# One activation-table set for all of ScalarE's functions in a two-layer graph attention kernel

## The chip, the cores and the metric

The kernel runs on one core of a Trainium2 chip. The metric is the device time of one execution in microseconds (us). The engines are named as in the profile: PE is TensorE (PEld its weight loads), DVE is VectorE, ACT is ScalarE, POOL is GpSimd, SP is SyncE, whose queue issues the plain DMAs.

## What is computed

Two layers, each an attention over a sparse graph of 2048 nodes with 256 features, a residual and a layer norm, all in float32:

```
q, k, v = x @ Wq.T, x @ Wk.T, x @ Wv.T
scores  = where(adj.T, q @ k.T, -1e30)
attn    = where(adj.T, softmax(scores, axis=1), 0)
x       = layernorm(x + attn @ v)          # eps 1e-5; done twice, with two sets of weights
```

An edge is there with probability 0.000977, so a node has two neighbours on average.

## The kernel before

The 2048 rows are 16 tiles of 128, handled as 8 pairs (p = 0 to 7) per layer. Dense scores are not computed. At the start (0 to about 62 us) PE packs the adjacency bits, DVE reads neighbour lists out of them, and POOL gathers neighbour rows with indirect DMAs. Each tile has two direct neighbour slots (xd, line 314, two gathers per tile) and one tile of "overflow" rows (xo, line 318, one gather) that holds the third and further neighbours.

One pair then goes through these steps, with lines of the kernel before:

1. PE turns two tiles of x (L935), ACT copies the result to xt (L371), PE multiplies by M = Wq^T Wk (L944), ACT copies it to Q (L380). In layer 0 the pairs 0 to 3 of layer 1 are prepared in this way inside the loop at p = 4 to 7, the next three behind the loop and the last at p = 0 of layer 1.
2. PE expands Q to the overflow edges (L1009); DVE multiplies and sums Q with xd and xo (L709, L716): the scores.
3. PE scatters edge scores to slots (L1021), DVE masks them and takes the maximum (L733, L740), ACT does the exponentials (exps, L416) and scales the first neighbour's row (first_row, L424); DVE adds the second (both_rows, L755).
4. PE takes the maximum to the edges (L1030), DVE subtracts (L747), ACT does the exponential (prob, L431) and scales own_t by it (weight, L435).
5. "Sums": PE adds both_rows and the weighted overflow rows (L1044, L1046), 8 matmuls in two passes each. ACT copies them to y_sb (L443), PE multiplies by Wv^T (L1056), DVE adds the residual (L775).
6. Layer norm: DVE computes mean and variance (L782, L790). ACT computes 1/sqrt(var + eps) as exp(-0.5 * ln(var + eps)): the logarithm at L451, the exponential (root) at L454. DVE makes off_mean (L799) and ACT scales the rows with Identity (L462). The very last but one tile is scaled by DVE (L806).

The steps are written out by hand for each engine and run in that order, with semaphores between the engines. ACT's order in one turn of the loop is: y_sb of pair p-1, X of p-3, xt, exps, first_row, prob, weight of p, logarithm and root of p-2, Q. At p = 2 of layer 0 copies of own_t (L392) and M (L366) follow, at p = 3 the copy of WvT (L366), for which PE waits before its next sums. Behind each layer's loop stands a tail with the norms of the last pairs. SP stores a pair's rows when it is normed, and POOL's gathers for layer 1 wait for the store of all rows of layer 0. From the fifth tile of layer 1 on (AHEAD = 4) a tile's gathers also wait for DVE's products of the tile four before.

ACT's functions on this path are Copy, Abs, Exp, Ln and Identity. The kernel before loads no table by name; the builder puts ACT_TABLE_LOAD instructions where it finds them needed, and their line is that of the ACTIVATE behind them.

A branch at each engine's end (too_many) handles graphs that overflow the lists; these inputs don't enter it.

Of the kernel before, what the change touches and what calls it, by code (L numbers as in the profile page):

```python
# [49 lines left out]
def edges_and_dense(nc, x, adj, wq, wk, wv, out):  # L50

    ctx = ExitStack()
    with ctx:
# [309 lines left out]
        def _(act):  # L363
            def weights(n, bank, into, nth):
                act.wait_ge(s["m_ps"], nth)
                act.activation(into[:, n, :, :], PS[:, bank, :].rearrange("p (h d) -> p h d", h=H), ACT.Copy).then_inc(s["m_sb"], 1)  # L366

            def rows_turned(z):

                act.wait_ge(s["xt_ps"], z + 1)  # L370
                act.activation(xt[:, z % 2, :, :, :], PS[:, 6, :].rearrange("p (j h n) -> p j h n", j=2, h=H),  # L371
                               ACT.Copy).then_inc(s["xt_sb"], 1)
# [16 lines left out]
            def own_turned(c):  # L389
# [3 lines left out]
                               ACT.Copy).then_inc(s["own_t_sb"], 1)  # L393

            weights(0, 4, M, 1)
            rows_turned(0)
            for z in range(1, 4):
# [4 lines left out]
            own_turned(0)  # L402
            own_turned(1)
            weights(0, 5, WvT, 2)
            for z in range(4, PAIRS):
                rows_turned(z)
# [58 lines left out]
            for layer in range(LAYERS):  # L465
                for p in range(PAIRS):
                    z = turned_for(layer, p)
                    if among(p - 1):
                        summed(layer, p - 1)
                    if among(p - 3):  # L470
                        normal(layer, p - 3)
                    if z is not None:
                        rows_turned(z)
                    exponents(layer, p)
                    first_rows(layer, p)
                    if layer == 0 and p == 1:
                        distances(1)
                    overflow_weights(layer, p)
                    if among(p - 2):
                        roots(layer, p - 2)  # L480
                    if z is not None:
                        queries(z)
                    if layer == 0 and p == 2:
                        own_turned(2)
                        own_turned(3)
                        weights(1, 7, M, 3)
                    if layer == 0 and p == 3:
                        weights(1, 6, WvT, 4)
# [692 lines left out]
```

## Time and profile before

| | us |
|---|---|
| median of 3 runs | 311.3 |
| lowest and highest | 307.36 and 314.35 |
| the profiled execution, its time | 310.94 |
| its span, first to last instruction | 309.1 |
| mean granted TensorE clock, share of full speed | 0.797 |
| ACT busy | 139.9 |
| DVE busy | 132.5 |
| POOL busy | 94.4 |

The span is what the profile shows; the execution's own time has 1.8 us more around it. Busy time of an engine is summed over its instructions, and says nothing on what waited for what. For that the timeline gives each instruction's start and duration, and in brackets how long its engine had been idle before it and whose signal ended that. Ends of matmuls are modelled, so an interval on PE is best read from start to start. A granted clock of 1.00 is 2.4 GHz, of 0.50 it is 1.2 GHz.

### The profile page before, as it was taken

What the parts mean: (1) busy time and instruction counts of PE and PEld (TensorE: products, weight loads), DVE (VectorE), ACT (ScalarE), POOL (GpSimd) and SP (SyncE); (2) the same over time, 40 slices, a digit from 0 to 9 for tenths busy, and PEclk for the clock granted to TensorE, in tenths of its full rate; (3) what the DMA queues carried; (4) which work ended last, traced back from release to release, by engine and by line L of the source; (5) the groups of instructions that cost most, each with busy time, mean ns of one, the idle gap of its engine ahead of it and who ended that gap; (6) DMA issues with size and microseconds to landing.
All of it is one profiled execution on the core that took longest, in us unless ns stands there. A gap on an engine that the chain in (4) does not pass through costs nothing.

```text
span 309.1 us, 3691 instructions
## 1 busy us (share of the span) xinstructions
PE 186.0 (60%) x1110; PEld 158.4 (51%) x1110; DVE 132.5 (43%) x671; ACT 139.9 (45%) x311; POOL 94.4 (31%) x115
## 2 busy tenths in 40 slices
PE   1739699640185879298878528650583285957640
PEld 1527587530174767197767426450473184946520
DVE  1229557010097780716874201240185063567430
ACT  1012143400124282739999772210245274688884
POOL 3457102777300036000000007776047315610000
PEclk9999685995556678879999968776599559597965
DMA  8999200433200004110011123333013204311112
GB/s 222 325 311 347 88 0 19 103 107 106 77 0 0 3 25 104 42 34 3 33 35 37 34 68 90 108 104 104 4 35 104 69 33 136 89 49 34 36 36 71
DMA packets 20982, 24.92 MB, mean 81 GB/s; under 512 B 2016, under 2 KB 17888, under 8 KB 20960
## 3 DMA queue, kind: packets, MB, share of 16 engines
q0 software_dynamic: 4608, 12.59, 15.0%
q1 hardware_dynamic: 16352, 12.06, 13.0%
q8 instruction: 11, 0.18, 0.2%
q14 instruction: 11, 0.09, 0.1%
HBM read 20.45 MB, written 4.19 MB: 80 GB/s over the span
## 4 chain that ended last, share of the span: by engine, by line
PE 33%; ACT 23%; issue 19%; another core or an unknown queue 16%; DVE 8%; ACTq 0%; DVEq 0%
PE PS L944 8%; PE PS L1056 7%; ACT L451 5%; PE PS L1044 3%; PE PS L1046 3%; PE PS L1009 3%; ACT first_row L424 3%; ACT exps L416 2%; PE PS L935 2%; ACT weight L435 2%; ACT L454 2%; ACT y_sb L443 2%; DVE X L775 1%; PE PS L918 1%
## 5 line engine op out<-in xcount | busy, mean ns | idle before, releaser
L1056 PE MATMUL PS<-WvT,y_sb 128*128 128x256 f32 x128 | 41.4, 456 | 33.0 <-ACT y_sb L443 32.3
L314 POOL DMA_INDIRECT xd<-x_rows,d_row x32 | 30.6, 957 | 98.6 <-DMA x_rows<-X 62.7
L1044 PE MATMUL PS<-ident,both_rows 128*128 128x128 f32 x128 | 32.6, 346 | 25.1 <-DVE both_rows L755 11.7
L944 PE MATMUL PS<-M,xt 128*128 128x256 f32 x128 | 39.5, 463 | 11.7 <-ACT xt L371 8.6
L1056 PEld LDWEIGHTS PS<-WvT,y_sb 128*128 128x128 f32 x128 | 26.0, 222 | 39.8 <-ACT y_sb L443 35.4
L775 DVE SCALAR_TENSOR_TENSOR X<-PS,inv,X 128x256 f32<-128x256 f32 x32 | 15.4, 483 | 66.9 <-PE PS L1056 62.2
L1044 PEld LDWEIGHTS PS<-ident,both_rows 128*128 128x128 f32 x128 | 26.2, 250 | 26.9 <-issue 19.5
L944 PEld LDWEIGHTS PS<-M,xt 128*128 128x128 f32 x128 | 28.4, 233 | 18.3 <-ACT xt L371 9.9
L314 POOL DMA_INDIRECT xd<-in_x,d_row x32 | 30.5, 955 | 18.5 <-DVE d_row L581 9.4
L709 DVE CUSTOM_DVE_ANT_0 prod<-Q,xd,d_none 128x256 f32<-128x256 f32 x64 | 28.4, 481 | 8.4 <-DMA xd<-x_rows,d_row 8.4
L318 POOL DMA_INDIRECT xo<-in_x,e_row x16 | 15.2, 952 | 54.5 <-DVE e_row L671 50.3
L1046 PE MATMUL PS<-weight,xo 128*128 128x128 f32 x128 | 31.5, 337 | 0.0
L416 ACT ACTIVATE exps<-slots,neg_top 128x18 f32<-128x18 f32 x32 | 9.6, 302 | 48.0 <-issue 26.4
L380 ACT ACTIVATE Q<-PS 128x512 f32<-128x512 f32 x16 | 9.5, 592 | 43.2 <-PE PS L944 21.8
L1046 PEld LDWEIGHTS PS<-weight,xo 128*128 128x128 f32 x128 | 25.9, 251 | 0.0
L716 DVE CUSTOM_DVE_ANT_0 prod<-PS,xo 128x256 f32<-128x256 f32 x32 | 13.4, 419 | 17.9 <-remote 16.3
L443 ACT ACTIVATE y_sb<-PS 128x512 f32<-128x512 f32 x16 | 9.5, 591 | 24.9 <-PE PS L1046 16.3
L451 ACT ACT_TABLE_LOAD x16 | 20.5, 1283 | 0.3
L454 ACT ACT_TABLE_LOAD x16 | 20.5, 1283 | 0.3
L1030 PEld LDWEIGHTS PS<-neg_top,own 128*128 128x128 f32 x64 | 11.1, 222 | 15.6 <-issue 13.5
L1009 PE MATMUL PS<-Q,own 128*128 128x256 f32 x64 | 18.9, 429 | 0.0
L1030 PE MATMUL PS<-neg_top,own 128*128 128x1 f32 x64 | 9.6, 254 | 14.0 <-issue 13.3
(125 smaller groups left out, 303.9 us busy)
## 6 DMA issues: line engine op xcount, KB each, us to landing
adj_words<-in_adj SPq DMA_DIRECT2D x4, 1024.0 KB, 7.1
X<-in_x SPq DMA_DIRECT2D x2, 1024.0 KB
x_rows<-X SPq DMA_DIRECT2D x7, 256.0 KB, 2.1
out<-X SPq DMA_DIRECT2D x7, 256.0 KB
W<-in_L_gnn_Wq SPq DMA_DIRECT2D x2, 256.0 KB
W<-in_L_gnn_Wk SPq DMA_DIRECT2D x2, 256.0 KB
xd<-in_x,d_row POOLq DMA_INDIRECT x32
W<-in_L_gnn_Wv SPq DMA_DIRECT2D x2, 256.0 KB
```

What stands on the lines that cost most here:

```text
L314: pool.indirect_dma_start(xd[:, t, k, :], None, rows, bass.IndirectOffsetOnAxis(ap=d_row[:, t, k:k + 1], axis=0)).then_inc(d_in[t], 16)
L416: act.activation(exps[:, n % 2, j, :], slots[:, n % 2, j, :], ACT.Exp, bias=neg_top[:, n % 2, j:j + 1], scale=-1.0, accum_out=total[:, t:t ...
L451: act.activation(log_var[:, :], moment[:, n % 2, :, 1], ACT.Ln, bias=eps[:, 0:1]).then_inc(s["logged"], 1)
L454: act.activation(root[:, n % 2, :], log_var[:, :], ACT.Exp, scale=-0.5).then_inc(s["rooted"], 1)
L709: dve.tensor_tensor_reduce(out=prod[:, i, :], in0=Q[:, t, :], in1=xd[:, t, k, :], op0=ALU.mult, op1=ALU.add, scale=-1.0, scalar=d_none[:, ...
L775: dve.scalar_tensor_tensor(out=X[layer + 1][:, t, :], in0=projected_into(j), scalar=inv[:, t:t + 1], in1=X[layer][:, t, :], op0=ALU.mult, ...
L944: last = nc.tensor.matmul(PS[:, 7, j * D:j * D + D], xt[:, z % 2, j, h, :], M[:, z // PAIRS, h, :], start=(h == 0), stop=(h == H - 1))
L1009: last = nc.tensor.matmul(expanded(n, j), own[:, 2 * p + j, :], Q[:, 2 * p + j, :], start=True, stop=True)
L1030: last = nc.tensor.matmul(edge_tops(n)[:, j:j + 1], own[:, 2 * p + j, :], neg_top[:, n % 2, j:j + 1], start=True, stop=True)
L1044: nc.tensor.matmul(PS[:, 4, at_h:at_h + P], both_rows[:, n % 2, j, h * P:h * P + P], ident[:, :], start=True, stop=False)
L1046: last = nc.tensor.matmul(PS[:, 4, at_h:at_h + P], xo[:, t, h * P:h * P + P], weight[:, n % 2, j, :], start=False, stop=True)
L1056: last = nc.tensor.matmul(projected_into(j), y_sb[:, n % 2, j, h, :], WvT[:, layer, h, :], start=(h == 0), stop=(h == H - 1))
```

## The change

ACT's program gets one statement at its head. It loads a table set by name, the one that holds logarithm, exponential and the copies, absolute value and identity.

```diff
@@ -364,6 +364,8 @@
             def weights(n, bank, into, nth):
                 act.wait_ge(s["m_ps"], nth)
                 act.activation(into[:, n, :, :], PS[:, bank, :].rearrange("p (h d) -> p h d", h=H), ACT.Copy).then_inc(s["m_sb"], 1)
+
+            act.preload_act_table_set("natural_log_exp_and_others")
 
             def rows_turned(z):
```

All lines behind it are two further down in the changed kernel (L451 becomes L453). What the builder makes of it is seen in ACT's order of instructions. At the head of ACT's program, before:

```order
L362 UNCONDITIONAL_BRANCH
L366 ACT_TABLE_LOAD
L366 ACTIVATE M<-PS 128x512
L371 ACTIVATE xt<-PS 128x512 x2
L380 ACTIVATE Q<-PS 128x512
```

The same place in the changed kernel:

```order
L362 UNCONDITIONAL_BRANCH
L368 ACT_TABLE_LOAD
L366 ACTIVATE M<-PS 128x512
L373 ACTIVATE xt<-PS 128x512 x2
L382 ACTIVATE Q<-PS 128x512
```

There is one load at the head in both, and it stands before the first wait in both. On ACT at the end of the turn p = 7 of layer 0 and in the tail behind it, before:

```order
L435 ACTIVATE weight<-own_t,prob 128x128 x2
L451 ACT_TABLE_LOAD
L451 ACTIVATE log_var<-moment,eps 128x2
L454 ACT_TABLE_LOAD
L454 ACTIVATE root<-log_var 128x2
L380 ACTIVATE Q<-PS 128x512
L462 ACTIVATE X<-X,off_mean,root 128x256 x2
L443 ACTIVATE y_sb<-PS 128x512
L451 ACT_TABLE_LOAD
L451 ACTIVATE log_var<-moment,eps 128x2
L454 ACT_TABLE_LOAD
L454 ACTIVATE root<-log_var 128x2
```

The same place in the changed kernel:

```order
L437 ACTIVATE weight<-own_t,prob 128x128 x2
L453 ACTIVATE log_var<-moment,eps 128x2
L456 ACTIVATE root<-log_var 128x2
L382 ACTIVATE Q<-PS 128x512
L464 ACTIVATE X<-X,off_mean,root 128x256 x2
L445 ACTIVATE y_sb<-PS 128x512
L453 ACTIVATE log_var<-moment,eps 128x2
L456 ACTIVATE root<-log_var 128x2
```

The loads before the logarithm and before the root are gone, at all 16 places where the two stand, 8 in each layer. Nothing else on the path of these inputs is added, removed or moved, on ACT or on another engine.

## Rows read from the trace of the kernel before

**Rows 1.** The page, part 1 (busy us, share, instructions) and part 4 (chain)

```profile
PE 186.0 (60%) x1110; PEld 158.4 (51%) x1110; DVE 132.5 (43%) x671; ACT 139.9 (45%) x311; POOL 94.4 (31%) x115
...
PE 33%; ACT 23%; issue 19%; another core or an unknown queue 16%; DVE 8%; ACTq 0%; DVEq 0%
```

**Rows 2.** Lines L451, L454: ns min/median/max, first and last start us

```profile
L451 ACT ACT_TABLE_LOAD  x16: 1283/1283/1283, 110.6 to 301.0; - x16
...
L454 ACT ACT_TABLE_LOAD  x16: 1283/1283/1283, 112.2 to 302.6; - x16
```

**Rows 3.** Timeline, layer 0, p = 5: start us, us, engine, line, operation, [idle before]

```profile
148.77 0.69 ACT L435 ACTIVATE weight<-own_t,prob 128x128 f32<-128x128 f32 x2
...
149.48 1.28 ACT L451 ACT_TABLE_LOAD   x1
...
150.77 0.30 ACT L451 ACTIVATE log_var<-moment,eps 128x2 f32<-128x2 f32 x1
...
151.01 0.39 PE L1046 MATMUL PS<-weight,xo 128*128 128x128 f32 x2
...
152.97 0.59 ACT L443 ACTIVATE y_sb<-PS 128x512 f32<-128x512 f32 x1
...
153.61 1.13 PE L1056 MATMUL PS<-WvT,y_sb 128*128 128x256 f32 x4 [0.91 <-ACT y_sb L443]
```

**Rows 4.** Timeline, layer 0, p = 2 to 4

```profile
114.27 3.78 PE L898 MATMUL PS<-W 128*128 128x256 f32 x8 [0.65 <-ACT own_t L392]
...
130.32 0.58 ACT L366 ACTIVATE WvT<-PS 128x512 f32<-128x512 f32 x1
...
130.95 0.80 PE L1044 MATMUL PS<-ident,both_rows 128*128 128x128 f32 x2 [4.99 <-ACT WvT L366]
...
134.53 1.68 PE L1009 MATMUL PS<-Q,own 128*128 128x256 f32 x4
...
140.83 0.38 PE L1044 MATMUL PS<-ident,both_rows 128*128 128x128 f32 x2
...
142.62 1.03 PE L1009 MATMUL PS<-Q,own 128*128 128x256 f32 x4
```

**Rows 5.** Timeline, layer 0, p = 6, p = 7 and the tail

```profile
162.22 1.13 PE L1056 MATMUL PS<-WvT,y_sb 128*128 128x256 f32 x4 [1.78 <-ACT y_sb L443]
...
171.81 1.99 PE L1056 MATMUL PS<-WvT,y_sb 128*128 128x256 f32 x8 [2.75 <-ACT y_sb L443]
...
175.41 1.99 PE L944 MATMUL PS<-M,xt 128*128 128x256 f32 x8 [1.61 <-ACT xt L371]
...
179.03 1.28 ACT L451 ACT_TABLE_LOAD   x1
```

**Rows 6.** Timeline, layer 1, the first two bursts of gathers, a later y_sb

```profile
185.15 0.95 POOL L314 DMA_INDIRECT xd<-x_rows,d_row  x1 [62.67 <-DMA x_rows<-X]
...
197.42 3.59 PE L944 MATMUL PS<-M,xt 128*128 128x256 f32 x8
...
214.14 0.95 POOL L318 DMA_INDIRECT xo<-x_rows,e_row  x1 [0.30 <-issue]
...
218.88 0.60 ACT L380 ACTIVATE Q<-PS 128x512 f32<-128x512 f32 x1 [15.03 <-remote]
...
241.61 0.95 POOL L318 DMA_INDIRECT xo<-x_rows,e_row  x1 [0.30 <-issue]
...
244.78 0.60 ACT L443 ACTIVATE y_sb<-PS 128x512 f32<-128x512 f32 x1 [8.42 <-remote]
...
266.64 0.60 ACT L443 ACTIVATE y_sb<-PS 128x512 f32<-128x512 f32 x1 [0.52 <-PE PS L1046]
```

**Rows 7.** Timeline of PE, layer 1, L1056 behind the loads of p = 5 and p = 7

```profile
277.85 1.13 PE L1056 MATMUL PS<-WvT,y_sb 128*128 128x256 f32 x4 [0.92 <-ACT y_sb L443]
...
295.64 3.21 PE L1056 MATMUL PS<-WvT,y_sb 128*128 128x256 f32 x8 [3.10 <-ACT y_sb L443]
```

**Rows 8.** Windows: stretch, us, busy of PE, PEld, DVE, ACT, POOL, clock, DMA

```profile
131.00:135.80 4.80, 4.80 (x19) 4.54 (x20) 0.27 (x1) 1.03 (x3) 0.00 (x0) 0.50 0.00 0
```

## The prediction

> **What bounds the kernel now.** I read the page first. No engine is busy for more than 60% of the span, and the chain that ended last is spread over PE 33%, ACT 23% and "issue" 19%, with 16% for releasers that the profile does not tell [rows 1]. So the time is a chain of hand-overs, and a duration counts where it stands in that chain, not in ACT's busy total. Then the groups of the two lines that carry table loads: 16 loads each at 1283 ns, the first at 110.6 us, the last at 302.6 [rows 2]. That is 32 x 1.283 = 41.1 us of ACT's time, all after 110 us. The question is how much of it is on the chain.
>
> Then the timeline of one pair in layer 0 [rows 3]. weight ends at 148.77 + 0.69 = 149.46, the load starts at 149.48, the logarithm 1.29 later, and y_sb starts at 152.97, without a hole in between. Whatever stands behind the loads in ACT's queue is late by up to two loads, 2.57 us. PE waits for that y_sb with L1056 (0.91 us idle), though its sums had ended at 151.01 + 0.39 = 151.40.
>
> **Whether a load costs more than its row.** The gap before the load is 0.02 us and that behind it 0.01 us [rows 3], so I price one at 1.283. The Trainium skill (ScalarE: Activation LUTs, "What ACT_TABLE_LOAD costs") adds a drain of 1.38 us to each load, 2.66 us per switch. By that the 32 switches would be 85 us of ACT, and the places below where ACT alone decides would give twice as much. The trace shows no drain, and the trace decides. The pair of ACTIVATEs stays: it was ordered by a semaphore before too (logged), whose delay is no more than the hand-over from load to ACTIVATE, so nothing new is exposed.
>
> **The change, part by part.** The load at the head stays one load at the head, before the first wait: 0. The 32 others go. I go through the places at which one of them is followed by a wait of another engine. A saving is the smaller of two things: what ACT delivers earlier, and how long the one who waits was idle.
>
> I name them by the turn p in whose queue the two loads stand. Layer 0 (p = 2 and 3 [rows 4], p = 5 [rows 3], p = 6, 7 and tail [rows 5]):
> - p = 2: PE waits 0.65 us for ACT's own_t before the product L898. The saving is 0.65.
> - p = 3: PE idles 4.99 us for ACT's WvT copy, which stands right behind the two loads. The sums behind it had their inputs before that. The saving is 2.57.
> - p = 4 and 5: y_sb could start when the sums end (151.40), 1.5 us earlier, but PE has its expand and transposes until 153.61 - 0.91 = 152.70. Two savings of 0.91, 1.8 in all. From there PE is the bound of the turn: 162.22 - 153.61 = 8.61 before, 7.7 us now.
> - p = 6: idle 1.78 us. The bounds are 0.9, as at p = 5, and 1.78. y_sb can't start before the sums end, and then needs some 0.7 us (0.59 and the hand-over), of which PE's transposes cover about 0.4. That leaves 0.3 of idle time and a saving of 1.5.
> - p = 7: L1056 idles 2.75 us. From the loads through Q, X and y_sb ACT has no hole, so all behind them moves up by 2.57, until y_sb meets the end of the sums: 2.5 (bounds 0 and 2.57).
> - Tail: PE's L944 idles 1.61 us for xt, behind the loads of pair 6: 1.6. Then the loads of pair 7 (179.03) stand on the path to the last rows stored: 2.57.
>
> Sum of layer 0: 0.65 + 2.57 + 1.8 + 1.5 + 2.5 + 1.6 + 2.57 = 13.2 us.
>
> Layer 1 begins with a burst of gathers on POOL at 185.15, released by the store of the last rows, so it moves with layer 0. Then it goes at the gathers' pace: one per 1.25 us (0.95 and 0.30 idle), 24 in the first burst, until 215.09 [rows 6]. PE's L944 started at 197.42 and ran 3.6 us, but the Q that reads it on ACT starts at 218.88, 3.8 us after the burst, with the releaser "remote". The same in the second burst: the last gather ends at 242.56, y_sb starts at 244.78 after 8.42 us idle. I read this as follows: PE's signals come late while a burst runs. The loads at p = 2 of layer 1 lie in the second burst, so they are worth 0. At p = 3 and 4 y_sb waits for PE's sums and not for ACT's queue (two rows such as the one at 266.64 [rows 6], ACT idle 0.5 us), so 0 again. Their cover is the burst and the sums; with it gone each could give 0.9 as p = 5 does, up to 2.57.
> - p = 5: L1056 idles 0.92 for y_sb [rows 7]: 0.9.
> - p = 6: taken as p = 3 and 4: 0 (bounds 0 and 0.9).
> - p = 7: L1056 at 295.64 idles 3.10. Without loads y_sb comes right after the sums, and the idle time falls to the 0.7 of a copy: 2.4 (bounds 0 and 2.57).
> - Tail: the loads of pair 6 run beside L1056 and the residual: 0. Those of pair 7 (301.0 and 302.6 [rows 2]) are on the path to the end: 2.57.
>
> Sum of layer 1: 5.9 us. Both: 19.1.
>
> **The clock.** In 131 to 135.8 us PE runs wholly at half rate (0.50), after the idle 4.99 us [rows 8]. In that stretch the sums take 134.53 - 130.95 = 3.58 us and expand 1.68. A turn later the same work takes 142.62 - 140.83 = 1.79 and 1.03 [rows 4]: 2.4 us less. Without loads the idle time is 4.99 - 2.57 = 2.4 us, less than the 2.75 before 171.81, where the L1056 behind it still took 1.99 us for 8 instructions [rows 5]. So I take the whole difference, 2.4 us (bounds 0 and 2.4). At the end L1056 took 3.21 for the same 8 instructions, after 3.10 idle [rows 7]. The idle time there shrinks to 0.7, so I take 3.21 - 1.99 = 1.2 (bounds 0 and 1.2). The Trainium skill (TensorE: Matmul & The Clock Gate, "What's actually happening") has idle as the throttled default, released by activity; that points the same way and also bears on the rival below, that fuller stretches gain still more.
>
> Together 19.1 + 3.6 = 22.7. The profiled execution took 310.9 us (span 309.1), close to the median 311.3. Forecast 310.9 - 22.7 = **288.2 us**. Two per cent of 311.3 is 6.2 us, about what runs of 307.4 to 314.4 can tell from no change.
>
> **The rivals.**
> - *The clock does not follow* (0.25): it falls for another reason than the one idle time. For it: L898 took 3.78 us for 8 instructions of L944's shape, which took 1.99 at 175.41, and it had idled just 0.65 [rows 4, 5]. Then 19.1 remains: 291.8.
> - *The bursts take more* (0.15). With layer 0 denser, signals held by a burst can fall on a worse step, such as the 8 overflow gathers under p = 2 and 3, or layer 1's first burst could hold back the products that its own seventh and eighth tile wait for. A hold that ends with a burst has cost 8.4 and 15.0 us [rows 6]. One more of the smaller size gives 288.2 + 8.4 = 296.6, one of the larger 303.
> - *More than the sum* (0.09): PE is denser from 128 us on, and a stretch in layer 1 goes at full clock too. Two further stretches such as the one priced at 2.4 give 283.4.
> - *The change doesn't take effect* (0.04): a load stays before each logarithm or each exponential. In the order of instructions none is left, which speaks against it. With loads in place it is 311.
> - *Slower: the common set reads more slowly* (0.02). The place is every ACTIVATE of the chain. The chain has ACT at 23% of 309.1 = 71 us [rows 1]; less the 22.7 priced above, 48 us of other ACT work is on it. If every ACTIVATE took longer with the new set, the gain would be gone at 22.7 / 48 = 47%, and it decides the sign from (22.7 + 6.2) / 48 = 60% on; with all of them doubled the time is 288.2 + 48 = 336. For it the trace has nothing but that the set is new to this kernel. The Trainium skill (ScalarE activation tables: per-element evaluation and per-set limits, "What a function is on this engine") says that with the same operands the instruction costs the same whichever table is read. No run so far shows it for this set.
>
> **How the numbers follow.** The forecast has 0.45. The range must leave out no more than 0.2: it takes in the forecast, the clock rival, most of "more than the sum" and the smaller hold, 283 to 299. Left out are the larger hold, the void change and the slow set. Faster by over 2% (under 305.1) holds for all but the last two and a little of the bursts: 0.93. Same 0.05, slower 0.02.
>
> **What would show it.** The lines of the logarithm and the exponential must have no loads, and ACT's busy time must fall from 140 to about 99 us. PE's idle time before L1056 in layer 0, p = 4 to 6, should be under 0.3 us, and the pairs 7.7 us apart. POOL's first gather of layer 1 should start near 185.15 - 15.6 = 169.5 us, and the stretch from there to y_sb of p = 5 should be as long as before. Wrong would be: the same ACTIVATEs at other durations, a half-rate stretch at the sums of p = 3, or a longer stretch of bursts.

## The result, and the profile after

The changed kernel took 286.1 us (median of 4 runs, 280.0 to 296.8) against 309.6 (4 runs, 307.4 to 314.4) of the kernel before on the same chip. The ratio is 0.912, 95% interval 0.898 to 0.926. It is faster. The forecast was 288.2; by the medians the gain is 23.5 us, by the ratio 27 us (of 309.6; by its interval 23 to 32), not 22.7. The ratio is made from undisturbed runs alone, of the changed kernel those of 280.0 and 283.2 us; the profiled one, 289.1, is not among them. The two profiled executions lie closer to it: the span fell from 309.1 to 287.4, by 21.7.

I read the page of the changed kernel first, parts 1 and 4, the rows that answer to [rows 1]:

```profile
PE 180.2 (63%) x1110; PEld 154.6 (54%) x1110; DVE 132.1 (46%) x671; ACT 97.9 (34%) x279; POOL 94.6 (33%) x115
...
PE 39%; another core or an unknown queue 27%; DVE 11%; issue 11%; ACT 9%; DVEq 0%
```

ACT lost 42.0 us and 32 instructions, as the change says. ACT's share of the chain fell from 23% to 9%. The share of releasers that the profile can't name ("another core or an unknown queue", in the timeline "remote") rose from 16% to 27%. After PE's 39% it is the largest part of the chain, and half of the experiments are about it. The lines of the logarithm and the exponential hold no load any more (the lines have moved down by two). The exponential lasts as long as before; the logarithm, which had stood behind a load, is 16 ns shorter (ns min/median/max; the first line is of the kernel before):

```profile
L451 ACT ACTIVATE log_var<-moment,eps x16: 295/296/297, 111.9 to 302.3; 128x2 f32<-128x2 f32 x16
...
L368 ACT ACT_TABLE_LOAD  x1: 1283/1283/1283, 0.8 to 0.8; - x1
...
L453 ACT ACTIVATE log_var<-moment,eps x16: 279/280/287, 112.2 to 281.7; 128x2 f32<-128x2 f32 x16
...
L456 ACT ACTIVATE root<-log_var x16: 203/203/204, 112.6 to 282.0; 128x2 f32<-128x2 f32 x16
```

Then the timeline of layer 0 at the places of [rows 3 to 5]:

```profile
129.06 0.58 ACT L366 ACTIVATE WvT<-PS 128x512 f32<-128x512 f32 x1
...
129.69 0.80 PE L1046 MATMUL PS<-ident,both_rows 128*128 128x128 f32 x2 [2.27 <-ACT WvT L366]
...
133.27 1.43 PE L1011 MATMUL PS<-Q,own 128*128 128x256 f32 x4
...
148.74 0.60 ACT L445 ACTIVATE y_sb<-PS 128x512 f32<-128x512 f32 x1 [1.06 <-PE PS L1048]
...
149.40 0.60 PE L937 MATMUL PS<-ident,X 128*128 128x128 f32 x4
149.84 1.03 PE L1058 MATMUL PS<-WvT,y_sb 128*128 128x256 f32 x4
...
156.90 1.13 PE L1058 MATMUL PS<-WvT,y_sb 128*128 128x256 f32 x4 [0.25 <-ACT y_sb L445]
...
163.98 1.99 PE L1058 MATMUL PS<-WvT,y_sb 128*128 128x256 f32 x8 [0.25 <-ACT y_sb L445]
```

The WvT copy comes sooner and PE's idle time before the sums fell from 4.99 to 2.27, yet the sums still take 133.27 - 129.69 = 3.58 us, the half-rate value. ACT now waits for PE before y_sb (1.06 us), where PE had waited for ACT. The idle time before L1058 is gone at p = 5 and 0.25 at p = 6 and 7, where it had been 0.91, 1.78 and 2.75.

Layer 1 of the same execution, to be held against [rows 6, 7]:

```profile
172.76 0.95 POOL L314 DMA_INDIRECT xd<-x_rows,d_row  x1 [48.53 <-DMA x_rows<-X]
...
184.59 3.11 PE L946 MATMUL PS<-M,xt 128*128 128x256 f32 x8
...
201.87 0.94 POOL L318 DMA_INDIRECT xo<-x_rows,e_row  x1 [0.31 <-issue]
...
205.74 0.60 ACT L382 ACTIVATE Q<-PS 128x512 f32<-128x512 f32 x1 [16.39 <-remote]
...
240.20 0.95 POOL L318 DMA_INDIRECT xo<-x_rows,e_row  x1 [0.30 <-issue]
...
243.37 0.60 ACT L445 ACTIVATE y_sb<-PS 128x512 f32<-128x512 f32 x1 [11.15 <-remote]
...
277.63 1.99 PE L1058 MATMUL PS<-WvT,y_sb 128*128 128x256 f32 x8 [0.69 <-ACT y_sb L445]
```

The first gather starts 12.4 us sooner than at 185.15. The two holds (a signal that comes long after the work it tells of) are still there: a Q that L946 had computed by 187.70 (184.59 + 3.11) is read at 205.74, 18.0 us later and 2.9 us after the run of gathers. It is the signals that are late and not the work: the sums of the same stretch have two halves, whose matmuls end 1.4 us apart at 191.25 and 192.61, and in the trace the semaphore updates of both come at 206.50 and 206.60. The last L1058 runs at full rate, 1.99 against 3.21 us.

Turn 2 of layer 0 is the first with loads, and its weight ends at 110.61 us before and 112.34 after, a difference that the loads can't have made. So I compare from there on. How much sooner each y_sb of layer 0 comes, counted from that point, and each event of layer 1, counted from its first gather (us, profiled pair, with the cumulative forecast):

```text
layer 0       y2    y3    y4    y5    y6    y7   first gather
forecast     0.65  5.62  6.5   7.4   8.9  11.4  15.6
measured     2.03  2.99  4.78  5.96  7.06  9.57 14.12
layer 1      y0 to y3   y4    y5    y6    y7   last X
forecast     0          0    0.9   0.9   3.3   7.1
measured    -1.6 to 5.7 0.3  2.7   3.2   5.6   9.5
```

The first gather had been forecast at 169.5 us and came at 172.8, of which 1.7 are the later start; the stretch from it to y5, forecast as long as before, is 2.7 shorter.

### The profile page after: what moved, and what is told of

It reads as the page before. It is cut to its first block, busy times and chain, and to the rows that moved or that the text cites. A ratio compares the mean times of both kernels' runs of the same rounds, so it can differ in the third digit from the quotient of the medians.

```text
span 287.4 us, 3659 instructions
## 1 busy us (share of the span) xinstructions
PE 180.2 (63%) x1110; PEld 154.6 (54%) x1110; DVE 132.1 (46%) x671; ACT 97.9 (34%) x279; POOL 94.6 (33%) x115
## 3 DMA queue, kind: packets, MB, share of 16 engines
q1 hardware_dynamic: 16352, 12.06, 14.1%
## 4 chain that ended last, share of the span: by engine, by line
PE 39%; another core or an unknown queue 27%; DVE 11%; issue 11%; ACT 9%; DVEq 0%
PE PS L1058 10%; PE PS L946 7%; PE PS L1046 6%; PE PS L1048 5%; PE PS L1011 4%; PE PS L1023 2%; DVE both_rows L757 1%; ACT y_sb L445 1%; ACT X L464 1%; PE PS L920 1%; PE PS L1032 1%; ACT first_row L426 1%; DVE prod L711 1%; ACT exps L418 1%
## 5 line engine op out<-in xcount | busy, mean ns | idle before, releaser
L1058 PE MATMUL PS<-WvT,y_sb 128*128 128x256 f32 x128 | 39.8, 441 | 24.7 <-ACT y_sb L445 23.9
L946 PE MATMUL PS<-M,xt 128*128 128x256 f32 x128 | 38.2, 451 | 7.7 <-ACT xt L373 5.2
L1058 PEld LDWEIGHTS PS<-WvT,y_sb 128*128 128x128 f32 x128 | 25.6, 218 | 30.7 <-ACT y_sb L445 26.3
L1046 PEld LDWEIGHTS PS<-ident,both_rows 128*128 128x128 f32 x128 | 25.6, 246 | 28.1 <-issue 16.6
L314 POOL DMA_INDIRECT xd<-in_x,d_row x32 | 30.5, 954 | 17.5 <-issue 10.1
L946 PEld LDWEIGHTS PS<-M,xt 128*128 128x128 f32 x128 | 27.0, 220 | 13.4 <-ACT xt L373 6.3
L1048 PE MATMUL PS<-weight,xo 128*128 128x128 f32 x128 | 30.8, 330 | 0.0
L1011 PE MATMUL PS<-Q,own 128*128 128x256 f32 x64 | 19.9, 448 | 0.0
L464 ACT ACTIVATE X<-X,off_mean,root 128x256 f32<-128x256 f32 x30 | 16.4, 591 | 4.7 <-DVE off_mean L801 4.7
L937 PE MATMUL PS<-ident,X 128*128 128x128 f32 x64 | 11.1, 302 | 10.9 <-issue 10.9
```

The lines of the kernel that those rows point to most:

```text
L314: pool.indirect_dma_start(xd[:, t, k, :], None, rows, bass.IndirectOffsetOnAxis(ap=d_row[:, t, k:k + 1], axis=0)).then_inc(d_in[t], 16)
L464: act.activation(xn, xn, ACT.Identity, bias=off_mean[:, n % 2, j:j + 1], scale=root[:, n % 2, j:j + 1]).then_inc(s["normed"], 1)
L946: last = nc.tensor.matmul(PS[:, 7, j * D:j * D + D], xt[:, z % 2, j, h, :], M[:, z // PAIRS, h, :], start=(h == 0), stop=(h == H - 1))
L1011: last = nc.tensor.matmul(expanded(n, j), own[:, 2 * p + j, :], Q[:, 2 * p + j, :], start=True, stop=True)
L1046: nc.tensor.matmul(PS[:, 4, at_h:at_h + P], both_rows[:, n % 2, j, h * P:h * P + P], ident[:, :], start=True, stop=False)
L1048: last = nc.tensor.matmul(PS[:, 4, at_h:at_h + P], xo[:, t, h * P:h * P + P], weight[:, n % 2, j, :], start=False, stop=True)
```

## The experiments

All kernels here are the changed one with an edit; the kernel before ran beside each set on the same chip. There are five sets, A to E, after the first letter of the labels. One thing has to be said ahead of them, because it decided what I ran: the kernels have two levels. In sets A, C and E the kernel before took 250.3, 250.4 and 250.1 us; in B and D, as on the first chip, 315.4 and 316.0. All its runs in a set agree within 4%. D and E are recorded under the same chip number, so I speak of the level of a set and not of a chip. The expectations still say chip.

Most edits put pairs of loads back where the kernel before had them. The edit is always this, with another condition:

```diff
@@ roots(layer, p), whose p is that of the turn less 2
+                if CONDITION:
+                    act.preload_act_table_set("natural_log")
                 act.wait_ge(s["spread"], 2 * (n + 1))
...
+                if CONDITION:
+                    act.preload_act_table_set("natural_log_exp_and_others")
                 act.wait_ge(s["logged"], n + 1)
```

**Set A: which layer's loads count (before 250.3 us).**

a1, no edit. 

> The changed kernel once more, for its spread and a second trace. Sum-of-places theory: 22.7 us under the kernel before (ratio 0.927). Theory that the gain is larger because bursts of gathers hold up less (rival): 26 to 28 us under it (ratio 0.912), and the two traces of the changed kernel differ in the idle time of the steps that wait for PE's signals in layer 1, not in layer 0's turns 4 to 7.

a2, CONDITION `layer == 0`. 

> The changed kernel with the two loads put back before logarithm and root in layer 0 alone (16 loads). Sum of places: layer 0's terms come back, 13.2 + 2.4 = 15.6 us over the changed kernel. Rival that every load is worth the same share of the gain (26 us / 32): 13 us. Rival that the gain is a matter of bursts in layer 1: under 10 us.

a3, CONDITION `layer == 1`. 

> The changed kernel with the loads put back in layer 1 alone (16 loads). Sum of places: 5.9 + 1.2 = 7.1 us over the changed kernel. Rival of equal shares: 13 us. Rival of bursts: over 10 us, and longer idle times of ACT and DVE that end by signals of PE.

a4, CONDITION `layer == 1 and p <= 2`, the six loads that the prediction priced at 0. 

> The changed kernel with loads back only at turns 2, 3 and 4 of layer 1 (6 loads), which the prediction priced at 0 because a burst of gathers or PE's sums cover them. Sum of places: 0 (bounds 0 and 2.7 us, three times 0.9). Equal shares: 5 us. If the cover is not there: up to 7.7 us.

```text
                     median us   ratio to before (95%)
a1 no loads           218.3      0.864 (0.858 to 0.869)
a2 loads in layer 0   239.3      0.958 (0.949 to 0.967)
a3 loads in layer 1   227.8      0.911 (0.905 to 0.916)
a4 six of them        221.2      0.885 (0.879 to 0.892)
```

The gain of the whole change is 32 us here by the medians and 34 by the ratio (0.136 of 250.3). Against a1, loads in layer 0 cost 21.0 us by the medians and 23.6 by the ratios, in layer 1 9.4 and 11.8, and the six "free" ones 2.8 and 5.4. The two layers' parts add up to the whole (30.4 of 32.0, 35.4 of 34.2), so they don't hide each other. The forecast's parts were 15.6 and 7.1: layer 0 costs more here than any of the three sizes that I had expected for a2. Against the trace of c1 below, from the weight of turn 2 to the first gather, a2 is 17.5 us longer (73.73 against 56.20) and from there to ACT's end another 2.7 (80.7 against 78.0); a3 is 6.5 us longer in that second part (84.5). In a4's trace the four turns from y0 to y4 of layer 1 take 33.5 us, in a1's and c1's 31.4 and 31.1.

**Set B: is it the chip, and what is a turn of layer 0 worth (before 315.4 us).**

b1, the kernel before itself. 

> The kernel before, profiled again, since the last job's chip ran it in 250 us and not in 310. Theory that the 60 us are signals of PE held up during bursts of gathers, a property of the chip and not of the kernel: here no ACT step idles over 5 us with the releaser 'remote' in layer 1, POOL issues its 48 gathers of layer 1 without a gap over 1 us, and the rest of the program (layer 0, turns 4 to 7, y_sb 8.61 us apart) is as in the first trace. Rival (everything is slower there, clocks or DMA): the same intervals differ in proportion, 8.61 becomes 7.

b2, no edit. 

> The changed kernel on the same chip. If the chip is one without holds: ratio 0.86, y_sb in layer 0 7.4 us apart; layer 1 bound by POOL's 48 gathers of 1.26 us. If it is one with holds: ratio 0.91.

b3, CONDITION `layer == 0 and p in (2, 3)`. 

> The changed kernel with the loads back at turns 4 and 5 of layer 0 alone (4 loads). The prediction's term (idle time of PE behind the modelled ends): 1.8 us over the changed kernel. Rival, PE read from start to start (8.61 to 7.44 per turn): 2.3 us. Rival of the whole load: 5.1 us.

b4, all of layer 1's gathers in one run:

```diff
-AHEAD = 4
+AHEAD = 16
```

> The changed kernel with AHEAD = 16: POOL's gathers of layer 1 no longer wait for DVE's products of the tile four before. On a chip without holds the throttle never bound: same time as the changed kernel (within 1 us). On a chip with holds: one burst of 60 us, and if PE's signals are held to its end, over 10 us slower.

b1 was to trace the kernel before on the level of 250 us, but the set ran on the other. It gave 319.3 us, ratio 1.009 (1.001 to 1.016): a difference of one per cent is not to be read here. b2 gave 296.3, ratio 0.935 (0.923 to 0.946), a gain of 21 us by the ratio and 19 by the medians; for a set with holds I had expected 0.91. b3 gave 302.3 (296.4 to 306.6), ratio 0.942 (0.930 to 0.955), so its total decides nothing against b2. Its trace does. Timelines of PE at turns 4 and 5, of b3:

```profile
149.92 1.13 PE L1062 MATMUL PS<-WvT,y_sb 128*128 128x256 f32 x4 [0.91 <-ACT y_sb L445]
...
158.53 1.13 PE L1062 MATMUL PS<-WvT,y_sb 128*128 128x256 f32 x4 [0.91 <-ACT y_sb L445]
```

and of b2:

```profile
147.78 1.03 PE L1058 MATMUL PS<-WvT,y_sb 128*128 128x256 f32 x4
...
155.22 1.03 PE L1058 MATMUL PS<-WvT,y_sb 128*128 128x256 f32 x4
```

The turn takes 8.61 us with the loads and 7.44 without: 1.17 us, where the idle time shown is 0.91. The rest is no idle time in the view: a row of PE begins before the modelled end of the one ahead of it (149.84 in the profile after, where the row before it ends at 149.40 + 0.60), and after an idle time it doesn't. So a saving of PE is to be read from start to start. Not all of it stays: from y3 to y6 b3 takes 24.8 us, b2 and the profile after 23.0 and 22.7, so the two pairs of loads cost 1.7 to 2.0 us there, near the 1.8 of the forecast.

b4 gave 310.9 us (305.0 to 316.9), 14.6 over b2 by the medians; its lowest two runs (305.0 and 305.2) are 11 us over those of b2 (293.8 and 294.4). Its 48 gathers run from 170.63 without a gap, and y_sb shows what it costs:

```profile
229.73 0.94 POOL L318 DMA_INDIRECT xo<-x_rows,e_row  x1 [0.30 <-issue]
...
238.17 0.60 ACT L445 ACTIVATE y_sb<-PS 128x512 f32<-128x512 f32 x1 [27.43 <-remote]
```

No tile gets through while the gathers run, and then the turns come 7.0 to 10.7 us apart. A longer run of gathers is a longer hold.

**Set C: the turn with the largest term, and the cover (before 250.4 us).**

c1, no edit. 

> The changed kernel once more, as the pair of the three that follow and for a trace in which to count PE's late signals. Holds theory: on a chip where no signal of PE is late outside the program's end the time is 214 to 222 us; where signals are late in the bursts it is 280 to 300 us, and the late ones are again PE's alone. Rival, that the chip's level comes from its clock or its DMA speed: the turns 4 to 7 of layer 0 would then differ between chips as the total does, by a fifth or more, and not stay at 7.4 us.

c2, CONDITION `layer == 0 and p == 1`. 

> Two loads back in turn 3 of layer 0 alone. Prediction's own term: 2.57 us for the WvT copy and 2.4 us for the half-rate stretch behind it, 5.0 together. Theory from the runs so far: on a chip without late signals y_sb of turn 3 comes about 4 us later than in the changed kernel (12.5 against 8.2 to 8.6 us after turn 2's); on one with late signals the turn is held anyway and the sums run at half rate in both, so 0 to 2.6 us. Rival, that the loads cost only their own time wherever they stand: 2.6 on either chip.

c3, layer 1's gathers left out; it reads the rows that layer 0 gathered:

```diff
-                direct(x1_dram, t)
-                overflow(x1_dram, t)
+                pass
...
-                        dve.wait_ge(d_in[t], 16 * S * (layer + 1))
+                        dve.wait_ge(d_in[t], 16 * S)
...
-                    dve.wait_ge(o_in[t], 16 * (layer + 1))
+                    dve.wait_ge(o_in[t], 16)
```

> Leaves out POOL's 48 gathers of layer 1; layer 1 reads the rows that layer 0 gathered (so its result is another). Theory, the gathers hold back PE's signals and pace layer 1: no signal of PE is over 1 us late in layer 1, its turns take 7.4 us as in layer 0, and from the first Q of layer 1 to the last y_sb there are 60 to 70 us; that is 40 to 60 us off the changed kernel's time on a chip with late signals, 8 to 20 us on one without. Rival, PE's signals are held by something else (stores, clock): holds of 8 to 18 us remain in layer 1 and under 15 us go.

c4, c3's edit and CONDITION `layer == 1 and p <= 2`. 

> Leaves out the same gathers and puts the six loads of turns 2 to 4 of layer 1 back, those that the prediction priced at 0 because bursts cover them. Cover theory: with the gathers gone these loads cost as in layer 0's turns 4 and 5, 1.2 us per turn in the trace, so 3.5 to 7.7 us in all over the kernel without gathers, on either chip. Rival, they are hidden behind PE in layer 1 in any case: under 1.5 us.

Medians: c1 219.4, c2 225.0, c3 217.7, c4 220.4. c1 is at the level of a1, and no signal of PE comes over 1 us late except at the program's end. Its turns 5 to 7 of layer 0 take 7.44, 7.49 and 7.09 us, those of b2 7.43, 7.52 and 7.09. So the 77 us between the levels are not an engine or a clock that is slower throughout, though the mean granted clock of b2 is lower (0.768 against 0.891).

c2 is 5.5 us over c1 (forecast for this turn: 4.97). In the traces the y_sb behind turn 3's loads comes 4.05 us later, counted from the weight of turn 2, and of the delay 3.8 us are left at the first gather. PE of c2:

```profile
99.41 0.80 PE L1050 MATMUL PS<-ident,both_rows 128*128 128x128 f32 x2 [4.85 <-ACT WvT L366]
99.99 0.64 PE L1052 MATMUL PS<-weight,xo 128*128 128x128 f32 x2
...
102.98 1.49 PE L1015 MATMUL PS<-Q,own 128*128 128x256 f32 x3
```

and of c1:

```profile
91.98 0.49 PE L1046 MATMUL PS<-ident,both_rows 128*128 128x128 f32 x2 [2.15 <-ACT WvT L366]
92.31 0.39 PE L1048 MATMUL PS<-weight,xo 128*128 128x128 f32 x2
...
93.42 0.62 PE L1046 MATMUL PS<-ident,both_rows 128*128 128x128 f32 x2
...
94.26 1.91 PE L1011 MATMUL PS<-Q,own 128*128 128x256 f32 x4
```

In c1 the idle time is 2.70 us shorter and the sums take 2.28 instead of 3.57 us: 1.3 us of clock, of the 2.4 priced. The windows of c1 show where it falls (stretch, us, busy of PE, PEld, DVE, ACT, POOL, granted clock, DMA):

```profile
88.00:91.90 3.90, 1.83 (x13) 1.49 (x12) 3.43 (x18) 3.23 (x12) 1.89 (x2) 1.00 0.61 168
91.90:94.30 2.40, 2.32 (x17) 2.32 (x18) 2.13 (x12) 0.03 (x1) 0.00 (x0) 0.82 0.02 7
94.30:96.50 2.20, 2.20 (x8) 1.73 (x8) 0.00 (x0) 1.57 (x3) 0.00 (x0) 0.50 0.00 0
```

The granted clock still goes to half rate; it does so in the middle of the sums and not before them. That is not the same in every execution. In a4 and e1 the same matmuls follow the same 2.15 us of idle time, and the clock stays at full rate through the sums (1.9 us) and the expand (1.03). Of a4:

```profile
93.57 0.49 PE L1050 MATMUL PS<-ident,both_rows 128*128 128x128 f32 x2 [2.15 <-ACT WvT L366]
...
95.45 1.03 PE L1015 MATMUL PS<-Q,own 128*128 128x256 f32 x4
```

```profile
93.50:95.40 1.90, 1.83 (x16) 1.83 (x17) 1.87 (x12) 0.01 (x1) 0.00 (x0) 1.00 0.00 0
```

There the next y_sb, y4, comes 5.2 us sooner than in c2 (23.37 against 28.54 from the weight of turn 2), in c1 3.8. So this turn's 4.97 lies between what two executions of the lower level give. In the profiled run of the changed kernel on the first chip PE had idled 2.38 us more before that, for neg_top:

```profile
126.30 0.61 PE L1032 MATMUL PS<-neg_top,own 128*128 128x1 f32 x4 [2.38 <-DVE neg_top L742]
```

and its windows show the clock fallen before the sums began:

```profile
126.00:129.50 3.50, 1.12 (x8) 0.86 (x8) 3.01 (x15) 3.13 (x12) 0.00 (x0) 0.68 0.02 9
129.50:133.30 3.80, 3.61 (x17) 3.61 (x18) 2.23 (x12) 0.14 (x1) 0.00 (x0) 0.50 0.00 0
```

c3: without the gathers of layer 1 the time hardly moves, 1.7 us by the medians, where I expected 8 to 20. So on this level the gathers don't bound layer 1. c4 is 2.8 us over c3 by the medians; from the first y_sb of layer 1 to the end it takes 3.8 us more, all of it in the four turns to y4. The runs of both spread over 6 us, so the trace carries this. (Ahead of these loads c4's first y_sb came 2.9 us sooner than c3's, which no edit explains, so from the last y_sb of layer 0 to the end only 0.9 us are left.) The rival, under 1.5, falls, and the size is the expected one (3.5) at its lower end. PE alone doesn't cover those loads.

**Set D: the same questions where signals come late (before 316.0 us).**

d1, no edit. 

> The changed kernel, as the pair of the three that follow. If PE's signals are late in the gather bursts on this chip it takes 280 to 300 us, and every late signal over 1 us lies inside a run of gathers; if none is late it takes 214 to 223 us. Rival: late signals of PE outside any gathers.

d2, c3's edit. 

> Leaves out POOL's 48 gathers of layer 1; layer 1 reads the rows that layer 0 gathered. On a chip without late signals the same as on the last one, 1 to 4 us under the changed kernel, since PE bounds layer 1 there. On a chip with late signals, if the gathers cause them: 30 to 50 us under it, with turns of 7.0 to 8.3 us and no late signal in layer 1. Rival, another cause: holds stay in layer 1 and it is under 15 us faster.

d3, CONDITION `layer == 1 and p <= 2`. 

> The six loads of turns 2 to 4 of layer 1 back in the changed kernel. Without late signals 3.4 to 5.4 us over it (3.4 in their turns with the gathers left out, 5.4 on another chip). With late signals the prediction's cover holds: 0 to 1.5 us. Rival, no cover even there: 3.4 or more.

d4, CONDITION `p >= 6`, in both layers. 

> The loads of pairs 6 and 7 back in both layers, eight of them, which stand in turn 8 and behind the last turn: the prediction's two tails, 1.6 + 2.57 us in layer 0 and 0 + 2.57 in layer 1, 6.7 together, on either chip, with 4.2 of it between layer 0's last y_sb and layer 1's first Q. Rival, the tails are hidden behind PE's own tail: under 3 us.

```text
                          median us   ratio to before (95%)
d1 no edit                  295.6     0.932 (0.912 to 0.951)
d2 no gathers in layer 1    252.3     0.800 (0.784 to 0.815)
d3 six loads under bursts   293.8     (none given)
d4 loads in the tails       305.0     0.955 (0.944 to 0.967)
```

d2 settles what the late signals of layer 1 come from: the gathers. Whether it is POOL's issuing or the transfers themselves, no run separates. The same edit that was worth 1.7 us in set C is worth 43.3 here. Q's group on ACT tells it (busy us, mean ns, idle us before and what ended it), of d1:

```profile
L382 ACT ACTIVATE Q<-PS 128x512 f32<-128x512 f32 x16 | 9.5, 593 | 46.6 <-remote 22.9 <-PE PS L946 19.6 <-issue 4.2
L445 ACT ACTIVATE y_sb<-PS 128x512 f32<-128x512 f32 x16 | 9.6, 597 | 41.6 <-PE PS L1048 27.3 <-remote 14.3
```

and of d2:

```profile
L381 ACT ACTIVATE Q<-PS 128x512 f32<-128x512 f32 x16 | 9.5, 592 | 29.1 <-PE PS L945 18.3 <-issue 6.9 <-remote 3.8
L444 ACT ACTIVATE y_sb<-PS 128x512 f32<-128x512 f32 x16 | 9.6, 597 | 30.2 <-PE PS L1047 27.2 <-remote 2.9
```

What is left under "remote" in d2 lies before 125 us, in layer 0, beside the gathers that stayed. In layer 1 no signal of PE is late: from the last y_sb of layer 0 to the first of layer 1 it is 24.1 us instead of 43.8, and from there to the last 52.6 instead of 72.9. In every trace with late signals they are PE's alone; a signal of DVE or ACT is nowhere late but at the program's end. Each of d1's comes inside a run of gathers (of either layer) or at most 4.2 us behind its end.

d3: the six loads cost nothing here, 1.9 us under d1 by the medians and 2.6 in the traces, which is within the spread. The same loads cost 2.8 us in set A by the medians, 5.4 by the ratios. A single pair of traces would not carry this, since layer 1 of the changed kernel differs by 7.5 us between traces of this level. But five of them agree: counted from the first gather, y4 comes at 81.5 and 81.9 us with loads (before, b1) and at 81.1, 82.2 and 80.8 without (after, b2, d1). The cover is real on this level, and it is the hold.

d4: the two tails cost 9.4 us by the medians (7.5 by the ratios), forecast 6.7. In the traces, from the last y_sb of layer 0 to the first gather it is 13.99 us instead of 9.43, so 4.6 (forecast 1.6 + 2.57 = 4.2), and from the last y_sb to the end of ACT's last ACTIVATE 8.99 instead of 6.06, so 2.9 (forecast 2.57). The waits are those of [rows 5] again:

```profile
169.95 1.99 PE L1062 MATMUL PS<-WvT,y_sb 128*128 128x256 f32 x8 [0.25 <-ACT y_sb L445]
173.56 1.99 PE L950 MATMUL PS<-M,xt 128*128 128x256 f32 x8 [1.62 <-ACT xt L373]
```

Another 3.2 us lie in the turns of layer 1 of these traces, where the holds fall at other places.

**Set E: shorter runs of gathers (before 250.1 us).** e1, `AHEAD = 2`. 

> AHEAD = 2 in the changed kernel: the gathers of layer 1 come in pairs of tiles at most, six at a time (7.5 us), and never 24. Theory, a hold ends with its burst: on a chip with late signals no signal is over 9 us late in layer 1, and the run of gathers takes 8 x (7.5 + 2 for the scores) = 76 us instead of 85, so 5 to 12 us under the changed kernel (ratio to before 0.89 to 0.92). On a chip without late signals the same pauses cost: 76 instead of 60 us of gathers, up to 16 us over the changed kernel. Rival, the pauses cost more than the holds do on either chip: slower on both.

e2, `AHEAD = 3`. 

> AHEAD = 3, between the two: the first run of gathers is 9 to 18 long. On a chip with late signals within 5 us of the changed kernel; without them the same to 8 us over it.

They took 221.6 us, ratio 0.900 (0.888 to 0.912), and 221.8 (no ratio given). This set ran at the lower level, without late signals, so it doesn't say what they were made for: whether shorter runs beat the changed kernel where signals are late. What it shows is the cost elsewhere: 2 to 3 us over the medians of a1 and c1, which ran in other sets, and by the ratios of e1 and a1 (0.900 and 0.864) 9 us. With AHEAD = 2 the gathers came in runs of 18, 18 and 12 and took 62.6 us, not 76, with two pauses of 1.3 and 1.4 us. My picture of eight runs of six was wrong. Neither is a better kernel as far as shown.

## Why the prediction was right or wrong

**Right.** The mechanism and the sign. All 32 loads were on ACT's queue ahead of something that others wait for; they are gone, ACT's ACTIVATEs cost the same (the logarithm 16 ns less), and PE has become the bound of layer 0's turns 5 to 7, with no more than 0.25 us of idle time before L1058. A load is worth its 1283 ns and no drain on top: a pair of loads moved WvT by 2.70 us (c1, c2). The Trainium skill's 2.66 us per switch (ScalarE: Activation LUTs, "What ACT_TABLE_LOAD costs") would be 5.3 for the pair; the trace of neither level shows it. The terms of p = 7 in layer 0 (2.5, measured 9.57 - 7.06 = 2.5), p = 7 in layer 1 (2.4, measured 2.4), both in the profiled pair, and the tails (4.2 and 2.6; measured 4.6 and 2.9 in d4) held. On the level of the first chip the sum held too. Two traces of the kernel before and three of the changed one give (us):

```text
            weight of turn 2   to first gather   to last X
before            110.6             74.5           119.8
b1, before        112.4             75.8           121.0
after             112.3             60.4           110.3
b2, after         116.9             61.3           117.8
d1, after         116.5             60.5           113.3
```

That is a mean gain of 14.4 us in the second column (forecast 15.6) and 6.6 in the third (7.1), 21.0 in all for 22.7; the medians of the three sets say 23.5, 19.1 and 20.3.

**The step that failed in the result: everything but the loads taken as fixed.** The forecast is one profiled execution less 22.7. It holds the time ahead of the first loads and the holds of layer 1 ("as long as before") at what that one trace has, and its rivals let the bursts cost more but never less. The range went 5.2 us below the forecast, to 283. The table shows how much those stretches move by themselves. The weight of turn 2, ahead of which no edit of these sets changes anything, ends at 110.8 (d2) to 120.3 us (b3) in eight traces of the changed kernel and its edits on this level, and layer 1 of the unedited changed kernel takes 110.3 to 117.8 us. The profiled run missed the forecast by 0.9 us; the runs that the ratio is made of, 280.0 and 283.2, lie 8.2 and 5.0 under it. What made those two quick is not shown, since there is no trace of them; that it lies in these stretches is an inference from their size.

**The step that fails on the other level: the cover over p = 2 to 4 of layer 1.** I read it in one trace and took it for a fact of the kernel. It is a fact of the level that the set runs at, and it did not miss in the first result. Where gathers hold PE's signals, these loads cost nothing that can be seen (d3, and y4 in five traces). Where they don't, they cost 2.8 to 5.4 us (a4) or 3.8 (c4's trace). The same change has a ratio of 0.912, 0.935 and 0.932 in three sets with late signals and 0.864 in one without (0.858 to 0.869). A reader of the forecast could not have expected the fourth.

**Mis-sized terms.** Turns 4 to 6 of layer 0: 3.3 us forecast, 4.1 measured in the pair (7.06 - 2.99), because I took idle time for the saving; the turn went to 7.44 us and not 7.7 (after, b2). At p = 2 I looked at L898 alone (0.65); y_sb of that turn stands behind the same loads and came 2.0 us sooner. At p = 3 I had 4.97, of which 2.4 for the clock. On the lower level it is 4.0 between c2 and c1: 2.7 of wait and 1.3 of clock. In the first pair it is 1.0, and the clock gave nothing; there neg_top was late too (2.38 us of idle PE). So the rival "the clock does not follow" was right there for this stretch: the sums ran at half rate in all ten traces of this level, behind idle times of 1.42 (d1) to 4.99 us. At p = 5 of layer 1 I had 0.9 and it is 2.4 in the profiled pair (2.7 less the 0.3 that y4 was ahead); between b1 and b2 it is 1.2, and d1 gains nothing there, so the pair's number is no measure of the term.

**Luck at the end.** The clock term of the last L1056, 1.2, came true in the profile after (3.21 to 1.99), but not for the reason given, the shorter idle time. In b2, a2 and c1 the same instructions took 3.78 us behind the same 0.69 us of idle time, in the other thirteen of the sixteen traces without loads there 1.99 or 2.00. Of c1:

```profile
205.43 3.78 PE L1058 MATMUL PS<-WvT,y_sb 128*128 128x256 f32 x8 [0.69 <-ACT y_sb L445]
```

**Both readings of the sum.** The profiled pair gives from the weight of turn 2 on 14.1 + 9.5 = 23.6 us, less 1.7 for the later start: 21.9, near the 22.7. Its parts come near it partly by luck: layer 0 falls 1.5 short, with the 2.4 of clock at p = 3 missing, and layer 1 gives 2.4 more than forecast. The runs of the changed kernel spread over 17 us (280.0 to 296.8) on the first chip.

**What else is open.** On the lower level, parts seen in traces are 20.2 (17.5 and 2.7) and 6.5 us, 27 together; the medians say 30 for the two parts and 32 for the whole. Some 5 us of a run's time lie before turn 2's weight, which ends near 78.5 us in c1 and a2 and near 83 in a1, a3, c2 and c3, whatever the edit; a mean over a few runs can shift by part of that. I have no trace of the kernel before on the lower level to close it. What switches the two levels is not shown either: the same kernel, unedited, ran at both.

## What to carry to other kernels

A table load that stands in an in-order queue costs its own duration wherever the next waiter has nothing else to do: look for one table set that holds all the functions. Read the saving of an engine from start to start of the same instruction in two turns, not from the idle column. Compare stretches that the change can't touch before a difference of a few us is given to the change. And a stretch that a wait of unknown origin covers is not free: price it twice, with the cover and without, since the cover may be gone the next time the kernel runs.

## What the hardware showed that I had not expected

Runs of indirect gathers on POOL can hold back PE's semaphore updates (18.0 us for L946 in the profile after, 16.7 in d1) while those of ACT and DVE come in time, and in sets A, C and E the same program shows no such thing. Without late signals the kernel before takes 250 us and with them 316; in d1 against c1, 38.5 us of the difference lie before the first y_sb, beside the gathers of layer 0, and 37.1 between the last y_sb of layer 0 and the last of layer 1. Gathers have the same duration in both (0.95 us, 0.30 between), and from y4 to y7 of layer 0 PE, DVE and ACT are busy for the same time within 0.3% in c1 and b2 (PE 44.2 us).

Of the clock: in c1 an idle 2.15 us ahead of the sums was followed by 1.4 us at full rate and then half rate; in a4 and e1 the same 2.15 us were followed by full rate all through; in the profile after, behind two idle times of 2.38 and 2.27 us, the sums ran wholly at half rate. The Trainium skill (TensorE: Matmul & The Clock Gate, "What's actually happening") has idle as the throttled default. The profile after agrees. The rows of c1 add that the fall can come in the middle of the work behind an idle time, and those of a4 that it can stay away; so a saving of clock is a chance and not a sum.
